# A fused routed-LoRA and masked FFN kernel: token products as 400 and 200 columns, and another order in the last pair

## The reference

```python
# x (8,256,1024); W, V (1024,1024); Wr (8,1024); A (8,16,1024); B (8,1024,16); cent (64,1024)
logits = x @ Wr.T + 5.0 * onehot(ids)[:, None]          # per token, 8 experts
gates  = softmax over the top 2, scattered to 8
h      = einsum('btd,erd->bter', x, A)
cond   = x @ W.T + 2.0 * einsum('bter,bte,eor->bto', h, gates, B)
dots   = softmax(cond @ cent.T / 0.1);  hits = dots > 0.01
row    = any(hits over clusters);  col = any(hits over tokens)[assignments]
out    = x + where(row & col, cond @ V.T + bias, 0)
```

## Time and profile before

| | |
|---|---|
| median of 3 runs | 345.57 us (345.12 to 345.95) |
| the profiled execution's own time | 345.21 us |
| its span | 343.2 us |
| granted PE clock, mean | 0.995 |
| PE / DVE / ACT busy | 335.8 / 254.4 / 134.9 us |
| sweep, one pass | 12.6 us |
| pairs begin | 161.06 us |
| last matmul starts | 336.92 us |
| last store issued | 340.65 us |

### The profile page before, as it was taken

The page is one execution under the profiler, slowest core; times in us unless marked ns, Lnnn a source line. Parts: engine busy times, 40 slices in busy tenths (PEclk is TensorE's granted clock), DMA queues, the critical chain, the costliest instruction groups (busy, mean ns, idle before and its releaser), DMA issues.

```text
span 343.2 us, 4823 instructions
## 1 busy us (share of the span) xinstructions
PE 335.8 (98%) x1887; PEld 295.5 (86%) x1887; DVE 254.4 (74%) x442; ACT 134.9 (39%) x218; POOL 1.0 (0%) x9
## 2 busy tenths in 40 slices
PE   8999999999999999999999999999999999999993
PEld 7888889999999999999887888888888888888882
DVE  3748965648779779779886979669397693985926
ACT  4744565245545554555534313222233222233020
POOL 1000000000000000000000000000000000000000
PEclk9999999999999999999999999999999999999997
DMA  7966341523533533414803180814608146060303
GB/s 214 413 204 251 109 162 61 155 100 116 178 97 102 178 116 102 153 61 158 334 1 124 61 302 36 285 52 164 206 0 308 61 155 212 2 244 0 124 0 122
DMA packets 14214, 49.11 MB, mean 143 GB/s; under 512 B 1712, under 2 KB 1712, under 8 KB 14192
## 3 DMA queue, kind: packets, MB, share of 16 engines
q1 hardware_dynamic: 14192, 48.80, 40.8%
HBM read 40.41 MB, written 8.39 MB: 142 GB/s over the span
## 4 chain that ended last, share of the span: by engine, by line
PE 97%; DVE 1%; issue 1%; ACT 0%; POOL 0%; POOLq 0%; DVEq 0%
PE ps L927 30%; PE ps L928 29%; PE ps L929 29%; PE ps L936 6%; PE ps L933 1%; PE ps L1003 1%; DVE u L840 0%; DVE u L904 0%; DVE u L816 0%; DVE nat L910 0%; DVE u L589 0%; ACT u L402 0%; PE ps L1065 0%; POOL ident L383 0%; PE ps L1059 0%
## 5 line engine op out<-in xcount | busy, mean ns | idle before, releaser
L927 PE MATMUL ps<-vt_hi,w_hi 128*128 128x288 f32 (+1 forms) x184 | 58.8, 319 | 0.0
L928 PE MATMUL ps<-vt_lo,w_hi 128*128 128x288 f32 (+1 forms) x184 | 58.0, 315 | 0.0
L929 PE MATMUL ps<-vt_hi,w_lo 128*128 128x288 f32 (+1 forms) x184 | 58.0, 315 | 0.0
L402 ACT ACTIVATE u<-ps 128x512 f32<-128x512 f32 x32 | 19.1, 598 | 88.4 <-PE ps L929 59.0
L928 PE MATMUL ps<-gop_lo,sl_s_hi 128*128 128x512 f32 x128 | 49.8, 389 | 0.0
L927 PE MATMUL ps<-gop_hi_t,sl_s_hi 128*128 128x512 f32 x96 | 37.5, 390 | 0.0
L929 PE MATMUL ps<-gop_hi_t,sl_s_lo 128*128 128x512 f32 x96 | 37.4, 389 | 0.0
L928 PEld LDWEIGHTS ps<-vt_lo,w_hi 128*128 128x128 f32 x184 | 34.6, 188 | 1.6
L927 PEld LDWEIGHTS ps<-vt_hi,w_hi 128*128 128x128 f32 x184 | 34.6, 188 | 1.6
L929 PEld LDWEIGHTS ps<-vt_hi,w_lo 128*128 128x128 f32 x184 | 34.5, 188 | 1.6
L927 PE MATMUL ps<-aw_hi,xt_hi 128*128 128x200 f32 x128 | 35.5, 277 | 0.0
(11 more groups left out here) (131 smaller groups left out, 683.4 us busy)
## 6 DMA issues: line engine op xcount, KB each, us to landing
xt_raw<-in_xt SPq DMA_DIRECT2D x32, 512.0 KB, 3.4
nat<-in_x SPq DMA_DIRECT2D x16, 512.0 KB, 3.8
out<-nat SPq DMA_DIRECT2D x15, 512.0 KB, 2.9
w_raw<-in_w SPq DMA_DIRECT2D x8, 512.0 KB, 3.3
wraw<-in_w SPq DMA_DIRECT2D x6, 512.0 KB, 4.3
vt_raw<-in_v SPq DMA_DIRECT2D x4, 576.0 KB, 5.4
vt_raw<-in_v SPq DMA_DIRECT2D x4, 256.0 KB, 5.3
wq_raw<-in_wq SPq DMA_DIRECT2D x4, 256.0 KB, 5.6
```

The costliest lines, as they stand in the source:

```text
L402: return nc.scalar.activation(dst, src, ACT.Copy)
L927: nc.tensor.matmul(dst, l_hi, r_hi, start=start, stop=False, skip_group_check=True)
L928: nc.tensor.matmul(dst, l_hi, r_lo, start=False, stop=False, skip_group_check=True)
L929: return nc.tensor.matmul(dst, l_lo, r_hi, start=False, stop=stop, skip_group_check=True)
```

## The change

- `aw_hi` and `aw_lo` become one tile `aw` of 400 columns: hi of A, Wr, centroids (200), then lo of the centroids (64), lo of A and Wr (136). A token product's k is one matmul of xt_hi with all 400 columns and one of xt_lo with the first 200. PSUM then holds two partial sums, 200 columns apart (h and router at `LO_A:LO_END`, logits at `AWG:LO_A`). The logits of `lora_logits` likewise: 128 and 64 columns with `gb`.
- The two halves are added on DVE. ACT first copies the second half to SBUF: `take_rest` (into `aw_rest`) and in `softmax_exp` (into `hits`). `route` adds two instructions, `softmax_max` one; `mx` and the exponentials read `hits`.
- In the sweep DVE does `split_hgt(n - 1)` ahead of `split_x(1, n)`.
- `turn_hg(7)` stands behind the first product of pair 0, no longer ahead of it.
- In the last pair the product with R21 and its lora come last, in two quarters (256 columns each, in two banks). Tile 0's columns 0 to 511 are masked and added in two parts: first the part kept from X, then, at the end, the quarters from PSUM. SP stores columns 512 to 1023, then the two quarters. In the pass of DVE before it tile 0 of pair 6 is finished first, `rest_s(7)` follows, tile 1 comes last.

```diff
-gb_hi = sb("gb_hi", [P, C], F32R)
-gb_lo = sb("gb_lo", [P, C], F32R)
+gb = sb("gb", [P, 2 * C], F32R)
...
-    aw_hi = sb("aw_hi", [P, KD, AWG], F32R, sweeps)
-    aw_lo = sb("aw_lo", [P, KD, AWG], F32R, sweeps)
+    aw = sb("aw", [P, KD, LO_END], F32R, sweeps)
...
-    sp.wait_ge(result[0], i + 1)
-    at = slice(2 * i * P, (2 * i + 1) * P)
-    sp.dma_start(out_t[at, 0:HALF], nat[i % 2][0][:, 0:HALF]).then_inc(out_stored[i % 2][0], 16)
-    sp.wait_ge(result[0], i + 2)
-    sp.dma_start(out_t[at, HALF:FO], nat[i % 2][0][:, HALF:FO]).then_inc(out_stored[i % 2][0], 16)
+    parts = [slice(HALF, FO), slice(0, QUARTER), slice(QUARTER, HALF)]
+    for n, cols in enumerate(parts):
+        sp.wait_ge(result[0], i + 2 + n)
+        sp.dma_start(out_t[2 * i * P:(2 * i + 1) * P, cols],
+                     nat[i % 2][0][:, cols]).then_inc(out_stored[i % 2][0], 16)
...
+    def take_rest(n):
+        for c in range(2):
+            act.wait_ge(aw_ready[c], n + 1)
+        if n >= 1:
+            act.wait_ge(router, ROUTER_STEPS * (n - 1) + 6)
+        copy(aw_rest[:], ps_aw(n)[:, :, LO_A:LO_END]).then_inc(rest_taken, 1)
+
     def router_exp(n):
-        act.wait_ge(router, ROUTER_STEPS * n + 4)
+        act.wait_ge(router, ROUTER_STEPS * n + 5)
         nc.scalar.activation(e2[:], diff[:], ACT.Exp).then_inc(e2_ready, 1)
 
     def keep_hgt(n):
...
         copy(hgt_hi[:], ps_hgt).then_inc(hgt_hi_done, 1)
 
     def softmax_exp(n):
-        act.wait_ge(soft, SOFT_STEPS * n + 2)
+        act.wait_ge(logits_ready, n + 1)
         if n >= 1:
-            act.wait_ge(soft, SOFT_STEPS * (n - 1) + 5)
+            act.wait_ge(soft, SOFT_STEPS * n)
+        copy(hits[:], ps_aw(n)[:, :, AWG:LO_A]).then_inc(logits_rest, 1)
+        act.wait_ge(soft, SOFT_STEPS * n + 3)
         for c in range(2):
-            nc.scalar.activation(ex[:, c, :], ps_aw(n)[:, c, AW:AWG], ACT.Exp, bias=negb[:, c:c + 1],
+            nc.scalar.activation(ex[:, c, :], hits[:, c, :], ACT.Exp, bias=negb[:, c:c + 1],
                                  scale=1.0 / TEMPERATURE, accum_out=esum[:, c:c + 1]).then_inc(exp_done, 1)
...
     for n in range(NPAIR):
         if n >= 1:
             split_x(0, n)
+            take_rest(n - 1)
...
-        aw = ps_aw(n)
-        for c in range(2):
-            dve.wait_ge(aw_ready[c], n + 1)
-        nc.vector.tensor_tensor(rl[:], aw[:, :, ER:AW], lang_bias[:, n:n + 1, :].broadcast_to([P, 2, E]),
+        sums = ps_aw(n)
+        dve.wait_ge(rest_taken, n + 1)
+        nc.vector.tensor_tensor(rl[:], sums[:, :, ER:AW], aw_rest[:, :, ER:AW], ALU.add).then_inc(router, 1)
+        dve.wait_ge(router, base + 1)
+        nc.vector.tensor_tensor(rl[:], rl[:], lang_bias[:, n:n + 1, :].broadcast_to([P, 2, E]),
                                 ALU.add).then_inc(router, 1)
-        dve.wait_ge(router, base + 1)
+        dve.wait_ge(router, base + 2)
         for c in range(2):
             nc.vector.max(m8[:, c, :], rl[:, c, :]).then_inc(router, 1)
-        dve.wait_ge(router, base + 3)
+        dve.wait_ge(router, base + 4)
         nc.vector.tensor_tensor(diff[:].unsqueeze(2), m8[:, :, 1:2], m8[:, :, 0:1],
                                 ALU.subtract).then_inc(router, 1)
...
+        nc.vector.tensor_tensor(hg[:], sums[:, :, 0:ER], aw_rest[:, :, 0:ER], ALU.add).then_inc(router, 1)
...
-                                aw[:, :, 0:ER].rearrange("p c (e r) -> p c e r", r=R),
+                                hg[:].rearrange("p c (e r) -> p c e r", r=R),
...
-        dve.wait_ge(logits_ready, n + 1)
-        nc.vector.tensor_reduce(mx[:], ps_aw(n)[:, :, AW:AWG], AX_X, ALU.max).then_inc(soft, 1)
+        dve.wait_ge(logits_rest, n + 1)
+        nc.vector.tensor_tensor(hits[:], ps_aw(n)[:, :, AW:AWG], hits[:], ALU.add).then_inc(soft, 1)
         dve.wait_ge(soft, base + 1)
+        nc.vector.tensor_reduce(mx[:], hits[:], AX_X, ALU.max).then_inc(soft, 1)
+        dve.wait_ge(soft, base + 2)
...
+        split_hgt(n - 1)
         split_x(1, n)
-        split_hgt(n - 1)
...
+        elif i == NPAIR - 1:
+            add22(i - 1)
+            add21(i - 1)
+            base(i - 1, 0)
+            add12(i - 1)
+            mask(i - 1, 0)
+            finish(i - 1, 0)
+            rest_s(i)
+            base(i - 1, 1)
+            mask(i - 1, 1)
+            finish(i - 1, 1)
...
     base(i, 0)
-    mask_last(0, f1, sum11)
+    dve.wait_ge(p1_kept, i + 1)
+    masked_to(u[:, 0, :], u[:, 0, :], f1).then_inc(masked[0], 1)
     base(i, 1)
-    finish_last(0, f1)
+    dve.wait_ge(masked[0], i + 1)
+    dve.wait_ge(based[0], i + 1)
+    nc.vector.tensor_tensor(at[:, f1], u[:, 0, :], at[:, f1], ALU.add).then_inc(result[0], 1)
...
     add12(i)
-    mask_last(1, f2, sum12)
-    finish_last(1, f2)
+    dve.wait_ge(sum12, i + 1)
+    masked_to(u[:, 1, :], u[:, 1, :], f2).then_inc(masked[0], 1)
+    dve.wait_ge(masked[0], i + 2)
+    nc.vector.tensor_tensor(at[:, f2], u[:, 1, :], at[:, f2], ALU.add).then_inc(result[0], 1)
+    dve.wait_ge(result[0], i + 1)
+    for h in range(2):
+        cols = slice(h * QUARTER, (h + 1) * QUARTER)
+        dve.wait_ge(y_bank, i + 1 + h)
+        masked_to(u[:, 0, cols], bank(i + h, BANK_Y)[:, cols], cols).then_inc(masked[0], 1)
+        dve.wait_ge(masked[0], i + 3 + h)
+        nc.vector.tensor_tensor(at[:, cols], u[:, 0, cols], at[:, cols], ALU.add).then_inc(result[0], 1)
...
-            last = three(ps_aw(n)[:, c, 0:AWG], xt_hi[c][:, k, :], xt_lo[c][:, k, :], aw_hi[:, k, :],
-                         aw_lo[:, k, :], k == 0, k == KD - 1)
+            nc.tensor.matmul(ps_aw(n)[:, c, 0:LO_END], xt_hi[c][:, k, :], aw[:, k, :], start=(k == 0),
+                             stop=(k == KD - 1), skip_group_check=True)
+            last = nc.tensor.matmul(ps_aw(n)[:, c, 0:AWG], xt_lo[c][:, k, :], aw[:, k, 0:AWG], start=False,
+                                    stop=(k == KD - 1), skip_group_check=True)
...
-            last = three(ps_aw(n)[:, c, AW:AWG], hgt_hi[:, t], hgt_lo[:, t], gb_hi[:], gb_lo[:], False, True)
+            nc.tensor.matmul(ps_aw(n)[:, c, AW:LO_A], hgt_hi[:, t], gb[:], start=False, stop=True,
+                             skip_group_check=True)
+            last = nc.tensor.matmul(ps_aw(n)[:, c, AW:AWG], hgt_lo[:, t], gb[:, 0:C], start=False, stop=True,
+                                    skip_group_check=True)
...
-    turn_hg(NPAIR - 1)
...
+            turn_hg(NPAIR - 1)
...
+    i = NPAIR - 1
+    pe.wait_ge(sa_split, i + 1)
+    pe.wait_ge(sum22, i - 1)
+    product(i, BANK_X, l11, R11, True).then_inc(x_bank, 1)
+    pe.wait_ge(s22_split, i + 1)
+    pe.wait_ge(sum21, i - 1)
+    product(i, BANK_V, l22, T4, True, False)
+    pe.wait_ge(hgm_split, i + 1)
+    lora21(i)
+    pe.wait_ge(ss_split, i + 1)
+    pe.wait_ge(p1_kept, i + 1)
+    product(i, BANK_X, s_of(S2), T2, False).then_inc(x_bank, 1)
+    pe.wait_ge(sum12, i - 1)
+    product(i, BANK_W, s_of(S1), T1, True).then_inc(w_bank, 1)
+    pe.wait_ge(u2_kept, i + 1)
+    product(i, BANK_X, s_of(S3), T3, False, False)
+    lora(i, BANK_X, 1, 1).then_inc(x_bank, 1)
+    pe.wait_ge(p5_kept, i + 1)
+    product(i, BANK_W, s_of(S4), R22, False, False)
+    lora(i, BANK_W, 0, 1).then_inc(w_bank, 1)
+    for h in range(2):
+        cols = slice(h * QUARTER, (h + 1) * QUARTER)
+        dst = ps[:, 4 * ((i + h) % 2) + BANK_Y, cols]
+        pe.wait_ge(sum11, i - 1 + h)
+        for k in range(KH):
+            l_hi, l_lo = l12(k)
+            three(dst, l_hi, l_lo, gop_hi_r[:, R21, k, cols], gop_lo[:, R21, k, cols], k == 0, False)
+        t = slice(0, P)
+        three(dst, hgm_hi[i % 2][:, t], hgm_lo[i % 2][:, t], gb3_hi[:, 0, cols], gb3_lo[:, 0, cols], False,
+              True).then_inc(y_bank, 1)
```

## The result

The changed kernel takes 339.28 us (median of 4 runs, 338.59 to 339.73); the kernel before, beside it on the same chip, 345.35 (344.99 to 345.95). The ratio is 0.9816, 95% interval 0.9800 to 0.9831: 6.1 us less, where 6.55 were forecast. The profiled execution took 339.44 with a span of 337.6.

A forecast was written before the change was run, and what follows sets the result against it. PE was taken to bound the kernel before, with DVE taking over from pass 2 after the change. 4.75 us from the sweep plus 1.8 from the tail made 6.55 less, a median of 339.0, range 334.5 to 342.0.

The forecast's parts named there:

- PE got shorter: Sweep on PE: token products 8.0 us less and logits 1.8, together 9.8; a pass from 12.59 to 11.37.
- the position of 94.75: Earlier PE timeline: a 200-column matmul behind a 288, successor 0.09 later; taken for each 200 behind a 400, 0.09 to 0.095.
- the second rival's case: Token-product matmuls not as short as said: 0.290 a group gives 339.5, 0.338 gives 342.6; chance 0.12.
- DVE became the bound: Sweep from pass 2 on: DVE needs 12.0 us a pass against PE's 11.37, so DVE sets the pace.
- x's rest: PE's wait for DVE's split_x at token_product(1, n), about 0.5 us, in the passes with t_sums.
- hg at the turn: PE's wait for DVE's hg at turn_hg in the sweep, 0.3 to 0.4 us.
- Ahead of T4: PE's wait for DVE's rest_22 before pair 0's product with T4: 1.7 us, the product starting 4.5 us earlier.
- ACT's copies hidden: ACT's two PSUM copies per pair, some 0.4 us each, cost nothing by themselves, as ACT idles 6 us a pass.
- The slower rival: ACT's copies never hidden in the sweep: DVE pass 13.1 us, kernel at 346.7; chance 0.05.
- The one that put the bound on PE: Rival: PE stays the bound in the sweep, all 9.8 us come plus 1.8, kernel at 334.0; chance 0.13.
- The gap between short matmuls: Token products on PE: short matmuls with a load each follow at 0.111 us; the skill's rule would make their gain nothing.
- The last pair: Tail after moving R21's product to the end in two quarters: 1.8 us less, bounds 1.3 and 2.2, bounded by DVE.

The follow-up runs named there:

- experiment 1: Kernel before with only the new token products, logits, halves added on DVE, moved split_hgt and turn_hg(7); last pair as before: 341.0 us against 345.75.
- experiment 3: Changed kernel without DVE's three adds of halves per pair, ACT's copies kept: 336.67 us, ratio 0.9736.
- experiment 4: experiment 3 with each k of the token product as two matmuls of 300 columns instead of 400 + 200: 334.77 us, ratio 0.9682.
- experiment 7: Changed kernel with the last product in one piece of 512 columns and one store of 256 KB: 338.88 us, ratio 0.9811.
- experiment 11: Changed kernel with route(7) moved into pair 0, its exponential ahead of x's copy, last product in one piece, hit_sum on GpSimd: 337.24 us, ratio 0.9753.

## Why the prediction was right, step by step

**PE got shorter, by less than forecast; this term was mis-sized.** The step was "the 200 behind it is in the position of 94.75, so 0.09 to 0.095", and so 0.271 a group and 8.0 us. Measured are 0.291 and 16 x (2.66 - 2.33) = 5.3 us, in the changed kernel's trace and in experiment 1's alike, which is the bound named beside it (0.290) and the second rival's case. The reading of the single starts was correct for the first group and no steady state: I took the row behind one long matmul for that behind each. Logits gave the 0.22 a pair that was said, 1.8 us (a pass in experiment 3 is 0.9 shorter than before, two token products of 0.33 and these 0.22). PE shed 7.1, not 9.8, and its own pass is 11.70, not 11.37.

**DVE became the bound, and this made up for it.** DVE's pass was forecast at 12.0, from its 25.2 less 2.7 of slack plus 2 x 0.86 less overlaps; measured 11.94, and experiment 3 shows that these adds are what PE waits for. Because both the forecast and the chip end at DVE's pace, the error of 2.7 on PE all but vanished: PE's waits are 2.7 us or so (1.1 in the passes, 1.6 ahead of T4; against experiment 3's trace, which loses 0.2 at T4 too, 2.3 are left by pair 1) where 4.9 were forecast (3.2 and 1.7). The rival with 0.290 a group gave 339.5 by this same account; it holds as to the mechanism, and 339.28 lies between it and the forecast. The logits of pass 1 and the gain of pair 0 are where the shorter matmuls would have counted, as said.

**Places of the waits.** x's rest: 0.34 and 0.33 lost in passes 4 and 6 (0.37 each against experiment 3's trace), forecast 0.5. hg at the turn: 0.06 to 0.07 in the odd passes from 3 on by the same comparison, forecast 0.3 to 0.4; with a longer PE the small wait there is the one that goes. Ahead of T4: 1.59, forecast 1.7. Along DVE the last `t_sums` began 4.5 earlier (150.55 - 55.42 against 154.31 - 54.70), forecast 4.7; from there to the rest that T4 needs it took 0.7 more, forecast 0.54. T4 began 4.2 earlier, forecast 4.5; pair 7 4.3 earlier, forecast 4.75. The missing 0.5 does not show in the medians of experiment 1, which gave 4.75, but it does in its trace (4.3). In the sum it is halved by the last pair, which gave 0.2 more than forecast: 4.3 + 2.0 against 4.75 + 1.8. This nearness is in part luck, as two small errors have opposite signs.

**ACT's copies hidden.** Right: experiment 3 keeps all 16, and PE waits for nothing in the sweep. The slower rival, which had them exposed, is out. The one that put the bound on PE (334.0) is out too, since PE does wait in the changed kernel; it had the mis-sized term besides, for even in experiment 3, with next to nothing for PE to wait for, it was 336.67.

**The gap between short matmuls.** The Trainium skill (TensorE: Matmul & The Clock Gate, Back-to-back issue gap) gives N/2.4 + 2.5 ns for an isolated matmul. The prediction set this against the rows and kept to the rows. By it the token products would have given nothing; they gave 5.3 us. The same section of the Trainium skill says that at small N this formula leaves out the weight load. The Trainium skill (TensorE: Matmul & The Clock Gate, LDWEIGHTS) gives a load P/1.2 ns; for 128 columns that is an estimate of 107 ns. The 0.11 pitch of the earlier trace rows agrees with it. A 200 streams faster than the next load is done; the next 400 can start at 0.08 to 0.09, but then its successor comes at 0.21, not 0.18. A group of 400 + 200 costs 0.017 more than two of 300, each of which covers a load. That the lost time is the load's is argued from these distances; experiment 4 shows that the alternation costs it, and no run takes the load apart.

**The last pair.** Forecast 1.8, measured 2.0 in the profiles and 2.1 alone. No wait at S2, as taken; rest_s(7) ended at 317.56 and S2 began at 317.94, a margin of 0.38 for the 0.4 forecast. The last store was issued 1.7 earlier than before, forecast 1.6, and landed in 1.7 rather than 2.3, a term that was on the careful side. The steps on the quarters were right in size, but against one whole piece they all but cancel, and 0.3 is left, from the landing: experiment 7.

## What to carry to other kernels

An engine at 98% can lose 7 us of work and the kernel still be set by one at 74%: what the second engine can give is its waits for the first one, not the rest of its span; list its waits by who ends them before counting on a gain. When two lists meet in several places, moving one wait moves the bill; look for the instruction that blocks the chain from the head of a third engine's list (here an exponential of 0.19 us behind a copy that waited 3.8 for a load). When a path gets shorter, see first what runs beside it: of 0.20 taken off DVE in experiment 11, 0.09 went to a copy on ACT that had been just in time. And read a pitch from a steady run of the same pattern, not from one row behind a different neighbour.

## What the runs showed of the hardware

- A short matmul behind a long one starts its successor early (0.08), and that one pays it back: 400, 200, 400 starts at 0.18, 0.08, 0.21, 0.09. At the same columns and loads 300 + 300 is 0.274 and 400 + 200 is 0.291.
- Beside an add on GpSimd (0.46), with 0.21 of overlap, DVE's two-input instruction of 1024 columns lasted 1.29 instead of 1.22. By these records it was not held back for the whole 0.21, and that of GpSimd is rough.
- A store's landing grows little with its size: in the changed kernel 512 KB 2.7 us (median of 15 over all pairs), 256 KB 2.0, 128 KB 1.7. Size isn't all: the last two of 256 KB in the kernel before had 2.5.
- A DVE instruction of 256 columns is 0.42 to 0.48 where 512 are 0.69 to 0.75, so halving one costs 0.15 to 0.21; on a tail bounded by DVE that takes up what the earlier start gives.
